# The column transform of the first pass with its weights and data exchanged, and the sums moved two slots on

## The chip, the core and the metric
The kernel runs as one program on 1 core of one Trainium2 chip. Its engines are TensorE (matmuls, into the accumulation memory PSUM), VectorE, ScalarE, GpSimd (POOL in the rows) and SyncE (SP), each with its own instruction queue; they wait for each other by semaphores. Transfers between main memory and on-chip memory run on 16 DMA engines. The metric is the time of one execution on the device in microseconds.

## The reference
The input `x` is 16 images of 64 channels of 256 x 256 fp32. Layer 0 normalizes `x` in groups of two channels, takes a two-dimensional real Fourier transform, keeps 32 x 17 modes of it, mixes the 16 channels of each of 4 heads with complex weights at each mode, transforms back and adds `x`:

```
x_freq = rfft2(gn(x)); xf = x_freq.reshape(B, 4, 16, fH, fW)
core = einsum('bhixy,hioxy->bhoxy', xf[:, :, :, :32, :17], weight)
x = x + irfft2(out_freq) + bias
```

Layer 1 normalizes again, applies a Lorentz-style normalization over the channels, for which it needs means over all images, and adds `x`.

## The kernel before, in words
Three passes run one after the other. Pass A (`stage_a`, lines 145 to 541) reads every image, computes its modes, mixes them and stores the mixed modes and the statistics. Pass B gathers the means over all images; pass C reads `x` a third time and writes the output. The change touches pass A alone.

**Tiles.** An image `b` is 8 tiles `q`, each with two channels of each head (2 MB, two DMAs of 1 MB, `load`, L210). Four buffers `xt` hold tiles, so tile `q` of an image takes the place of tile `q - 4`.

**TensorE, a slot per tile** (`slot`, L298). `row_dft(b, q)` transforms along the rows: 8 matmuls with 64 columns of weights and 512 moving, in pairs that write PSUM partitions 0 to 63 and 64 to 127; the profile has two records for each fp32 matmul. `transposes` then turns the copied rows of tile q-1 (8 records), and `col_dft` makes the modes of tile q-2: 8 matmuls (16 records) whose weights are 128 columns of data and whose moving operand is the 34 columns of the transform matrix, so that the modes come out with (head, row mode) on the partitions, 34 values for each of two channels. In slot 2 of image b TensorE also does `first_sums(b-1)` (two matmuls over squares and mean modes, L278) ahead of the column transform, and `second_sums(b-2)` (over the energy of the mixed modes, L287) at its end.

**ScalarE, a tile at a time** (`tile`, L347). Four activations sum the squares of the tile; between them ScalarE copies the rows (`copy_rows`, L333, two halves) and the transposed rows (`copy_tr`, L339, two halves) out of PSUM. After eight tiles `keep` (L360) copies the sums of squares.

**VectorE** (`entry`, L484). For each q it copies the modes of one tile out of PSUM (`copy_cols`, L384) and does one eighth of the mixing of the image before (`mix`, L390: a product and a reduction). After the eight of image b follow, in this order: `finish(b-1)` (L399: the rotated modes, L404 and L405, then the energy, L406 to L410), `first_norm(b)` (waits for first_sums(b)), `second_norm(b-1)` (waits for second_sums(b-1)) and `start(b)`, which scales the modes that the next eight products use. `mean_sum` (L436) after the first product waits for two powers by GpSimd.

**SP's queue** (L200 to L237) issues everything that is loaded, in program order. In the loop over the images b from 2 on, the store of the mixed modes stands between the loads of tile 3 and tile 4:

```
for q in range(Q):
    if q == 4:
        store_modes(b - 2)
    load(b, q)
```

`store_modes(b - 2)` (L205) begins with a wait for the two instructions L404 and L405 of `finish(b - 2)`. A load waits until TensorE and ScalarE are through with the tile that it overwrites. Waits of SP on register values have line 111.

Of the kernel before, what the change touches and what calls it, by code (L numbers as in the profile page):

```python
# [144 lines left out]
def stage_a(nc, ctx, io, B):  # L145
# [7 lines left out]
    const_in, w_in, neg_w = sem("const_in"), sem("w_in"), sem("neg_w")  # L153
    rows_mm, rows_sb = sem("rows_mm"), sem("rows_sb")
    tr_mm, tr_sb = sem("tr_mm"), [sem(f"tr_sb{i}") for i in range(2)]
    cols_mm, cols_sb = sem("cols_mm"), sem("cols_sb")
    sq_done, sq_kept = sem("sq_done"), sem("sq_kept")
    sums_mm, energy, stat_mm = sem("sums_mm"), sem("energy"), sem("stat_mm")
    y_ready, y_out, st_ready, st_out, chain = sem("y_ready"), sem("y_out"), sem("st_ready"), sem("st_out"), sem("chain")
    sums_read, stat_read = sem("sums_read"), sem("stat_read")  # L160
    var1_ready, rstd1_ready, var2_ready, yrot_out = sem("var1_ready"), sem("rstd1_ready"), sem("var2_ready"), sem("yrot_out")
    chain_end, macc_out, powers = sem("chain_end"), sem("macc_out"), sem("powers")

    with ExitStack() as mem:
# [10 lines left out]
        wm = sb("wm", [128, CI, 2, CI * M2])  # L175
        rows = [[sb(f"rows{a}{i}", [128, 512]) for i in range(2)] for a in range(2)]
        cols = [[sb(f"cols{a}{i}", [128, 512]) for i in range(2)] for a in range(2)]
        junk = [sb(f"junk{k}", [128, 1024], BF16) for k in range(2)]
        sq = sb("sq", [128, Q, HEADS])
        sqk = sb("sqk", [128, Q, HEADS])  # L180
# [8 lines left out]
        st = sb("st", [128, 4, CI])  # L189
        p_rows = [ps(f"p_rows{i}", [128, 512]) for i in range(2)]  # L190
        p_tr = [ps(f"p_tr{i}", [128, 512]) for i in range(2)]
        p_cols = [ps(f"p_cols{a}", [128, 2, M2]) for a in range(2)]
        p_sums = ps("p_sums", [128, 512])
        p_stat = ps("p_stat", [128, 512])
        consts = ((dft_h, "dft_h"), (dft_w, "dft_w"), (sel, "sel"), (mode_w, "mode_w"), (misc, "misc"), (ident, "ident"))

        block = mem.enter_context(nc.Block())
# [41 lines left out]
        @block.tensor  # L239
        def _(pe):  # L240
            def row_dft(b, q):

                pe.wait_ge(x_in[q % NX], b * 64 + (q // NX) * 32 + 32)
                for i in range(2):
                    if not (is_at(b, 0) and q == 0):
                        pe.wait_ge(rows_sb, b * 16 + 2 * q + i - 1)
                    for j in range(2):
                        for t in range(2):
                            last = nc.tensor.matmul(p_rows[i][64 * t:64 * t + 64, :], dft_h[:, j], xt[q % NX][:, t::2, i, j * W:(j + 1) * W],  # L249
                                                    start=(j == 0), stop=(j == 1))  # L250
                    last.then_inc(rows_mm, 1)

            def transposes(b, q):
                for i in range(2):
                    pe.wait_ge(rows_sb, b * 16 + 2 * q + i + 1)
                    if not (is_at(b, 0) and q == 0):
                        pe.wait_ge(tr_sb[i], b * 8 + q)
                    for hl in range(2):
                        for wh in range(2):

                            out = p_tr[i][:].rearrange("p (w r h k) -> p w h r k", w=2, r=2, h=4)[:, wh, 2 * hl:2 * hl + 2]
                            last = nc.tensor.transpose(out, rows[q % 2][i][:, 256 * hl + 128 * wh:256 * hl + 128 * wh + 128], ident[:])
                    last.then_inc(tr_mm, 1)

            def col_dft(b, q):
                if not (is_at(b, 0) and q < 2):
                    pe.wait_ge(cols_sb, b * 8 + q - 1)
                for i in range(2):
                    pe.wait_ge(tr_sb[i], b * 8 + q + 1)
                    v = cols[q % 2][i][:].rearrange("p (w r n) -> p w r n", w=2, r=2)  # L270
                    n = 0
                    for wh in range(2):
                        for r in range(2):
                            last = nc.tensor.matmul(p_cols[q % 2][:, i], v[:, wh, r], dft_w[:, r, wh], start=(n == 0), stop=(n == 3))
                            n += 1
                last.then_inc(cols_mm, 1)

            def first_sums(b):  # L278

                pe.wait_ge(sq_kept, b + 1)  # L280
                pe.wait_ge(cols_sb, b * 8 + 8)
                if not is_at(b, 0):
                    pe.wait_ge(sums_read, b)
                nc.tensor.matmul(p_sums[:, 0:32], sel[:, 0], sqk[:].rearrange("p q h -> p (q h)"), start=True, stop=True)
                nc.tensor.matmul(p_sums[:, 32:48], sel[:, 1], xm[:, :, 0], start=True, stop=True).then_inc(sums_mm, 1)

            def second_sums(b):  # L287

                pe.wait_ge(energy, b + 1)
                if not is_at(b, 0):  # L290
                    pe.wait_ge(stat_read, b)
                nc.tensor.matmul(p_stat[:, 0:16], sel[:, 2], sm[:, 8], start=True, stop=True)
                nc.tensor.matmul(p_stat[:, 16:32], sel[:, 1], y[:, :, 0], start=True, stop=True).then_inc(stat_mm, 1)

            def before(b, q, n):
                return (b, q - n) if q >= n else (b - 1, q - n + Q)

            def slot(b, q):  # L298
                row_dft(b, q)
                transposes(*before(b, q, 1))  # L300
                if q == 2 and not is_at(b, 0):
                    first_sums(b - 1)
                col_dft(*before(b, q, 2))
                if q == 2 and not (is_at(b, 0) or is_at(b, 1)):
                    second_sums(b - 2)

            pe.wait_ge(const_in, 32 + 16 * 8)
            row_dft(0, 0)
            row_dft(0, 1)
            transposes(0, 0)  # L310
            for q in range(2, Q):
                slot(0, q)
            for q in range(Q):
                slot(1, q)
            with pe.Fori(2, B) as b:
                for q in range(Q):
                    slot(b, q)
            transposes(B - 1, Q - 1)
            col_dft(B - 1, Q - 2)
            col_dft(B - 1, Q - 1)  # L320
            first_sums(B - 1)
            second_sums(B - 2)
            second_sums(B - 1)

        @block.scalar
        def _(act):
# [12 lines left out]
            def copy_tr(b, q, i):  # L339
# [4 lines left out]
                    act.wait_ge(cols_mm, b * 8 + q - 1)  # L344
                nc.scalar.activation(cols[q % 2][i][:], p_tr[i][:], ACT.Copy).then_inc(tr_sb[i], 1)

            def tile(b, q):  # L347
                act.wait_ge(x_in[q % NX], b * 64 + (q // NX) * 32 + 32)
                squares(b, q, 0)
                squares(b, q, 1)  # L350
                copy_rows(b, q, 0)
                if not (is_at(b, 0) and q == 0):
                    copy_tr(b, q - 1, 0)
                squares(b, q, 2)
                if not (is_at(b, 0) and q == 0):
                    copy_tr(b, q - 1, 1)
                squares(b, q, 3)
                copy_rows(b, q, 1)
# [11 lines left out]
            with act.Fori(1, B) as b:  # L370
                for q in range(Q):
                    tile(b, q)
                keep(b)
            for i in range(2):
                copy_tr(B - 1, Q - 1, i)

        @block.vector
        def _(dve):
# [2 lines left out]
            pair = lambda a: a.rearrange("p (g i) -> p g i", i=2)  # L381
            V = nc.vector

            def copy_cols(b, q):  # L384
                dve.wait_ge(cols_mm, b * 8 + q + 1)
                if q == 0 and not is_at(b, 0):
                    dve.wait_ge(sums_mm, b)
                V.tensor_copy(xm[:, 2 * q:2 * q + 2], p_cols[q % 2][:]).then_inc(cols_sb, 1)

            def mix(q, waited=None):  # L390

# [67 lines left out]
            def start(b):  # L459
# [8 lines left out]
                ch.step(V.tensor_scalar(row(7, 8), row(7, 8), misc[:, 4:5], None, ALU.mult))  # L468
                dcs = pair(xh[:, 0, 0::2])
                ch.step(V.tensor_tensor(dcs, dcs, row(7, 8).unsqueeze(2).to_broadcast((128, 8, 2)), ALU.add))  # L470
            ch.inc(V.memset(row(20), 0.0))
            ch.inc(V.memset(y[:, :, M2:YS], 0.0))
            ch.inc(V.memset(yrot[:, :, M2:YS], 0.0))
            dve.wait_ge(const_in, 32 + 16 * 8)
            for q in range(Q):
                copy_cols(0, q)
                if q == 5:
                    dve.wait_ge(w_in, 16)
                    neg = wm[:, :, 0].rearrange("p o (n r) -> p o n r", r=2)[:, :, :, 1]
                    ch.inc(V.tensor_scalar(neg, neg, -1.0, None, ALU.mult))  # L480
            first_norm(0)
            start(0)

            def entry(b, last=False):  # L484
                for q in range(Q):
                    copy_cols(b, q)
                    mix(q, None if is_at(b, 1) or q else (b - 1) * 16)
                    if q == 0 and not is_at(b, 1):
                        mean_sum(b - 2)
                finish(b - 1)  # L490
                first_norm(b)
                second_norm(b - 1)
                start(b)
# [48 lines left out]


PER_A = 47

TB = 4096
TC = 2048
# [823 lines left out]
```

## Time and profile before

| | |
|---|---|
| Time, median of 3 runs | 3578.98 us (3571.15 to 3595.31) |
| Profiled execution, its own time | 3573.87 us |
| Its span | 3572.3 us |
| Pass A | about 0 to 1030 us |
| Busy in the span: TensorE, VectorE, ScalarE, GpSimd | 2887.4, 2648.6, 2158.7, 1541.4 us |
| Mean DMA rate | 339 GB/s |
| VectorE's product L394 and its reduction L397 | 128 each, 2416 and 2421 ns |
| TensorE's row transform L249 | 2048 records, 515.7 us busy |
| Squares L330 on ScalarE | 512, 1055 ns each |

In the rows below, a timeline merges equal neighbouring instructions (x8 is eight of them, with their common start and length). A bracket at its end is the idle time of the engine before it and who ended that. PE is TensorE, DVE VectorE, ACT ScalarE. A busy TensorE is not at its peak; its clock is read from the granted share, 1.00 for the full level (2.4 GHz) and 0.50 for half of it.

### The profile page before, as it was taken

To read this page: it belongs to the slowest core of one execution; us is meant where nothing else is said; L and a number is where in the kernel's file an instruction comes from. 1 tells how busy PE (TensorE), PEld (TensorE's weight loads), DVE (VectorE), ACT (ScalarE), POOL (GpSimd) and SP (SyncE) were. 2 spreads that over 40 slices of the span, in tenths; PEclk is the share of its full clock that TensorE was granted. 3 is DMA by queue.
4 is the path that set the end of the run, shared out by engine and by line. 5 is a ranking of instruction groups with operands and counts; after the bars stand their busy time and mean duration, and the time that the engine had idled before them with its cause. 6 is when DMAs were issued, how large, how long until landed. Compare 5 with 4: busy or idle time off the path is not lost. (4 is left out here: it accounts for less than half of the span.)

```text
span 3572.3 us, 69803 instructions
## 1 busy us (share of the span) xinstructions
PE 2887.4 (81%) x26018; PEld 1418.3 (40%) x26018; DVE 2648.6 (74%) x2600; ACT 2158.7 (60%) x2994; POOL 1541.4 (43%) x862
## 2 busy tenths in 40 slices
PE   6999999999617567777671898888888889888887
PEld 3555555555402122222220544444444444444443
DVE  0788888888866635645562698888888888888888
ACT  6998888888500101101110788777787778777777
POOL 0112121111211112112211688777787777777777
PEclk9999999999759788887885899999999999999999
DMA  9888797979349899999994799999999999999998
GB/s 377 298 292 315 276 329 272 330 274 326 126 149 400 314 380 407 397 389 392 400 376 98 289 383 389 368 377 382 376 379 368 374 373 367 377 369 381 378 377 338
DMA packets 293208, 1211.31 MB, mean 339 GB/s; under 512 B 35265, under 2 KB 49798, under 8 KB 210694
## 3 DMA queue, kind: packets, MB, share of 16 engines
q1 hardware_dynamic: 263526, 1152.42, 84.4%
q0 software_dynamic: 14112, 43.37, 3.7%
q10 hardware_dynamic: 15360, 12.60, 1.2%
q8 instruction: 148, 2.42, 0.3%
q14 instruction: 62, 0.51, 0.0%
HBM read 883.89 MB, written 324.31 MB: 338 GB/s over the span
## 5 line engine op out<-in xcount | busy, mean ns | idle before, releaser
L1297 POOL TENSOR_TENSOR c_ot<-c_ot,c_pp 128x1024 f32<-128x1024 f32 x512 | 1214.7, 2374 | 409.7 <-DVE c_ot L1250 408.5
L1240 DVE SCALAR_TENSOR_TENSOR c_xt<-c_xt,keep_k,c_p_u 128x1024 f32<-128x1024 f32 x512 | 653.8, 1277 | 124.8 <-PE c_p_u L1120 97.5
L1250 DVE SCALAR_TENSOR_TENSOR c_ot<-c_p_f,keep_k,c_xt 128x1024 f32<-128x1024 f32 x512 | 657.2, 1284 | 117.8 <-DMA out<-c_ot 69.6
L1194 ACT ACTIVATE c_pp<-c_p_p,keep_cols 128x1024 f32<-128x1024 f32 x512 | 571.2, 1116 | 262.8 <-PE c_p_p L1132 261.4
L1120 PE MATMUL c_p_u<-c_mv,c_zc 64*128 64x256 f32 x4096 | 595.0, 410 | 74.8 <-DVE c_xt L1240 73.0
L1201 ACT ACTIVATE c_sq<-c_xt,keep_cols 128x1024 f32<-128x1024 f32 x512 | 583.3, 1139 | 60.0 <-DVE c_xt L1240 59.8
L330 ACT ACTIVATE a_junk<-a_xt 128x1024 bf16<-128x1024 f32 x512 | 537.7, 1055 | 26.6 <-DMA a_xt<-in_x 19.4
L249 PE MATMUL a_p_rows<-a_xt,a_dft_h 128*64 128x512 f32 x2048 | 515.7, 647 | 36.5 <-DMA a_bias_t<-in_bias 18.5
L1120 PEld LDWEIGHTS c_p_u<-c_mv,c_zc 64*128 64x128 f32 x4096 | 361.1, 190 | 353.8 <-issue 211.2
L1132 PE MATMUL c_p_f<-c_rt,keep_lw 64*128 64x512 bf16 x1024 | 313.0, 386 | 114.1 <-DVE c_ot L1250 101.6
L516 POOL TENSOR_TENSOR a_sm<-a_sm 128x8 f32<-128x8 f32 x16 | 26.8, 1672 | 806.4 <-DVE a_sm L457 806.4
L655 PE MATMUL b_p_al<-b_xt,b_awc 128*32 128x512 f32 x2048 | 292.0, 646 | 102.2 <-DMA b_xt<-in_x 102.0
L1132 PE MATMUL c_p_p<-c_rt,keep_lw 64*128 64x512 bf16 x1024 | 316.3, 390 | 0.0
L397 DVE TENSOR_REDUCE a_y<-a_prod 128x68 f32<-128x2176 f32 x128 | 309.9, 2421 | 5.6
L394 DVE TENSOR_TENSOR a_prod<-a_wm,a_xh 128x2176 f32<-128x2176 f32 x128 | 309.3, 2416 | 0.3
L713 ACT ACTIVATE b_dn<-b_dn,b_minus 128x512 f32<-128x512 f32 x16 | 11.6, 723 | 488.6 <-DVE b_dn L841 488.6
L816 DVE TENSOR_TENSOR b_prod<-b_spt,b_arow 64x2176 f32<-64x2176 f32 x16 | 38.7, 2418 | 335.0 <-DMA b_spt<-spec 334.9
L1143 PE MATMUL c_p_t<-c_sq,c_hw 128*32 128x512 f32 x2048 | 284.9, 629 | 1.3 <-ACT c_sq L1201 1.3
L655 PE MATMUL b_p_ls<-b_xt,b_awc 128*32 128x512 f32 x2048 | 283.4, 628 | 0.0
L1106 PEld LDWEIGHTS c_p_z<-c_idft,c_ys 128*37 128x37 f32 x7936 | 232.3, 114 | 105.6 <-issue 105.6
L1106 PE MATMUL c_p_z<-c_idft,c_ys 128*37 128x64 f32 x7936 | 271.4, 221 | 0.0
L249 PEld LDWEIGHTS a_p_rows<-a_xt,a_dft_h 128*64 128x64 f32 x2048 | 136.4, 147 | 307.9 <-issue 187.9
(205 smaller groups left out, 3032.0 us busy)
## 6 DMA issues: line engine op xcount, KB each, us to landing
a_xt<-in_x SPq DMA_DIRECT2D x256, 1024.0 KB, 8.8
b_xt<-in_x SPq DMA_DIRECT2D x128, 2048.0 KB, 16.8
c_xt<-in_x SPq DMA_DIRECT2D x256, 1024.0 KB, 16.2
out<-c_ot SPq DMA_DIRECT2D x256, 1024.0 KB, 16.5
c_rt<-maps SPq DMA_DIRECT2D x256, 96.0 KB
maps<-b_maps ACTq DMA_DIRECT2D x192, 64.0 KB, 13.5
maps<-b_maps POOLq DMA_DIRECT2D x64, 192.0 KB, 9.4
dmap<-b_dmap POOLq DMA_DIRECT2D x16, 768.0 KB, 13.5
```

The lines of the kernel that those rows point to most:

```text
L249: last = nc.tensor.matmul(p_rows[i][64 * t:64 * t + 64, :], dft_h[:, j], xt[q % NX][:, t::2, i, j * W:(j + 1) * W], start=(j == 0), stop=( ...
L330: nc.scalar.activation(junk[h % 2][:].rearrange("p (i w) -> p i w", i=2), xt[q % NX][:, h], ACT.Square, accum_out=sq[:, q, h:h + 1]).then_ ...
L397: ch.step(V.tensor_reduce(y[:, 2 * q:2 * q + 2, 0:M2].rearrange("p o (a k) -> p o a k", a=2), prod[:].rearrange("p o a (k n) -> p o a k n" ...
L655: last = nc.tensor.matmul(out[32 * j:32 * j + 32, :], awc[:, par, kind, 15 - k:47 - k], xt[t % NX][:, at:at + 512], start=(k == 0), stop=F ...
L1106: last = nc.tensor.matmul(p_z[64 * at:64 * at + YS, 64 * c:64 * c + 64], ys[:, 8 * part + c], idft[:, chunk, at], start=True, stop=True)
L1120: last = nc.tensor.matmul(p_u[:, 512 * at + W * r:512 * at + W * r + W], zc[t // CH][64 * at:64 * at + 64, i], mv[t % NB][64 * at:64 * at ...
L1132: last = nc.tensor.matmul(p[:, 512 * k:512 * k + 512], keep["lw"][at:at + 64, b].rearrange("p c s -> p (c s)"), rt[t % NB][at:at + 64, c:c ...
L1194: S.activation(pp[n][:], p_p[:], ACT.Identity, bias=keep["cols"][:, b, 1:2]).then_inc(pp_done, 1)
L1201: S.activation(sq[t % 2][:, 1024 * n:1024 * n + 1024], xt[t % NB][:, 1024 * n:1024 * n + 1024], ACT.Square, scale=keep["cols"][:, b, 0:1]) ...
L1240: V.scalar_tensor_tensor(out=u, in0=u, scalar=kc, in1=p_u[:], op0=ALU.mult, op1=ALU.add).then_inc(u_done, 1)
L1250: V.scalar_tensor_tensor(out=ot[t % NB][:, at], in0=p_f[:], scalar=kinv, in1=xt[t % NB][:, at], op0=ALU.add, op1=ALU.mult).then_inc(f_done, 1)
L1297: P.tensor_tensor(o, o, pp[n][:], ALU.add).then_inc(o_done, 1)
```

## The change
The column transform now has the 34 columns of the transform matrix as weights and the 128 columns of data moving. The two channels' results go to PSUM partitions 0 to 33 and 64 to 97 of one tile, `p_cm`. As the modes then lie on the partitions, ScalarE copies them (`copy_cm`, 98 partitions x 128), and one transpose per tile, `turn`, brings them back into `p_turn`, four tiles to a buffer. VectorE copies four tiles at once (`copy_half`), twice an image. `first_sums` and `second_sums` move from slot 2 to slot 4, the first of them to the slot's beginning, and the sums share one PSUM buffer. SP's program is not in the diff.

```diff
-            p_cols = [ps(f"p_cols{a}", [128, 2, M2]) for a in range(2)]
-            p_sums = ps("p_sums", [128, 512])
-            p_stat = ps("p_stat", [128, 512])
+            p_cm = ps("p_cm", [128, 512])
+            p_turn = [ps(f"p_turn{a}", [128, 512]) for a in range(2)]
+            p_stats = ps("p_stats", [128, 512])
+            p_sums, p_stat = p_stats[:, 0:64], p_stats[:, 64:96]
...
             def col_dft(b, q):
-                if not (is_at(b, 0) and q < 2):
-                    pe.wait_ge(cols_sb, b * 8 + q - 1)
+                if not (is_at(b, 0) and q == 0):
+                    pe.wait_ge(cm_sb, b * 8 + q)
                 for i in range(2):
                     pe.wait_ge(tr_sb[i], b * 8 + q + 1)
-                    v = cols[q % 2][i][:].rearrange("p (w r n) -> p w r n", w=2, r=2)
-                    n = 0
-                    for wh in range(2):
-                        for r in range(2):
-                            last = nc.tensor.matmul(p_cols[q % 2][:, i], v[:, wh, r], dft_w[:, r, wh], start=(n == 0), stop=(n == 3))
-                            n += 1
+                v = [cols[q % 2][i][:].rearrange("p (w r n) -> p w r n", w=2, r=2) for i in range(2)]
+                n = 0
+                for wh in range(2):
+                    for r in range(2):
+                        for i in range(2):
+                            last = nc.tensor.matmul(p_cm[64 * i:64 * i + M2, 0:128], dft_w[:, r, wh], v[i][:, wh, r],
+                                                    start=(n == 0), stop=(n == 3), skip_group_check=True)
+                        n += 1
                 last.then_inc(cols_mm, 1)
+            def turn(b, q):
+                pe.wait_ge(cm_sb, b * 8 + q + 1)
+                if q % 4 == 0 and not is_at(b, 0):
+                    pe.wait_ge(cols_sb, b * 2 + q // 4 - 1)
+                at = 128 * (q % 4)
+                nc.tensor.transpose(p_turn[q // 4][:, at:at + CM], cm[q % 2][:], ident[0:CM, 0:CM]).then_inc(turn_mm, 1)
             def first_sums(b):
                 pe.wait_ge(sq_kept, b + 1)
-                pe.wait_ge(cols_sb, b * 8 + 8)
+                pe.wait_ge(cols_sb, b * 2 + 2)
                 if not is_at(b, 0):
                     pe.wait_ge(sums_read, b)
+                    if not is_at(b, 1):
+                        pe.wait_ge(stat_read, b - 1)
...
             def second_sums(b):
                 pe.wait_ge(energy, b + 1)
+                pe.wait_ge(sums_read, B if is_at(b, B - 1) else b + 2)
...
             def slot(b, q):
+                if q == 4 and not is_at(b, 0):
+                    first_sums(b - 1)
                 row_dft(b, q)
                 transposes(*before(b, q, 1))
-                if q == 2 and not is_at(b, 0):
-                    first_sums(b - 1)
+                if not (is_at(b, 0) and q < 3):
+                    turn(*before(b, q, 3))
                 col_dft(*before(b, q, 2))
-                if q == 2 and not (is_at(b, 0) or is_at(b, 1)):
+                if q == 4 and not (is_at(b, 0) or is_at(b, 1)):
                     second_sums(b - 2)
...
+            def copy_cm(b, q):
+                if q < 0:
+                    b, q = b - 1, q + Q
+                act.wait_ge(cols_mm, b * 8 + q + 1)
+                if not (is_at(b, 0) and q < 2):
+                    act.wait_ge(turn_mm, b * 8 + q - 1)
+                nc.scalar.activation(cm[q % 2][:], p_cm[0:CM, 0:128], ACT.Copy).then_inc(cm_sb, 1)
             def tile(b, q):
                 act.wait_ge(x_in[q % NX], b * 64 + (q // NX) * 32 + 32)
                 squares(b, q, 0)
+                if not (is_at(b, 0) and q < 3):
+                    copy_cm(b, q - 3)
                 squares(b, q, 1)
...
-            def copy_cols(b, q):
-                dve.wait_ge(cols_mm, b * 8 + q + 1)
-                if q == 0 and not is_at(b, 0):
+            def copy_half(b, half):
+                dve.wait_ge(turn_mm, b * 8 + 4 * half + 4)
+                if half == 0 and not is_at(b, 0):
                     dve.wait_ge(sums_mm, b)
-                V.tensor_copy(xm[:, 2 * q:2 * q + 2], p_cols[q % 2][:]).then_inc(cols_sb, 1)
+                V.tensor_copy(xm[:, 8 * half:8 * half + 8], p_turn[half][:].rearrange("p (n m) -> p n m", m=64)[:, :, 0:M2]).then_inc(cols_sb, 1)
...
             def entry(b, last=False):
                 for q in range(Q):
-                    copy_cols(b, q)
+                    if q == 5:
+                        copy_half(b, 0)
                     mix(q, None if is_at(b, 1) or q else (b - 1) * 16)
                     if q == 0 and not is_at(b, 1):
                         mean_sum(b - 2)
+                copy_half(b, 1)
                 finish(b - 1)
                 first_norm(b)
                 second_norm(b - 1)
```

Before its first copy VectorE zeroes `p_cm`. After the last slot the remaining turns and copies follow in the same order.

## Rows read from the trace of the kernel before

**Rows 1.** Busy time by stretch: start:end, length, PE, PEld, DVE, ACT, POOL, PEclk, DMA share, GB/s

```profile
100.70:906.00 805.30, 767.32 (x4593) 438.02 (x4591) 683.41 (x858) 698.18 (x1359) 135.01 (x53) 0.94 0.83 298
...
391.00:392.00 1.00, 1.00 (x4) 0.24 (x2) 0.86 (x8) 0.00 (x0) 0.63 (x1) 0.50 1.04 404
```

**Rows 2.** Timeline of an ordinary slot, PE and ACT: start, length, engine, line, operation

```profile
402.35 1.09 PE L262 MATMUL a_p_tr<-a_ident,a_rows 128*128 128x128 f32 x8
403.28 1.87 PE L274 MATMUL a_p_cols<-a_dft_w,a_cols 128*128 128x34 f32 x16
405.08 3.68 PE L249 MATMUL a_p_rows<-a_xt,a_dft_h 128*64 128x512 f32 x16
408.69 0.55 PE L262 MATMUL a_p_tr<-a_ident,a_rows 128*128 128x128 f32 x3
...
402.40 0.60 ACT L337 ACTIVATE a_rows<-a_p_rows 128x512 f32<-128x512 f32 x1
403.12 0.60 ACT L345 ACTIVATE a_cols<-a_p_tr 128x512 f32<-128x512 f32 x1
...
406.17 0.60 ACT L337 ACTIVATE a_rows<-a_p_rows 128x512 f32<-128x512 f32 x1
```

**Rows 3.** Timeline of PE, from slot 2 to slot 4

```profile
384.16 1.95 PE L274 MATMUL a_p_cols<-a_dft_w,a_cols 128*128 128x34 f32 x16
388.72 0.60 PE L292 MATMUL a_p_stat<-a_sm,a_sel 128*128 128x16 f32 x2 [2.61 <-DVE a_sm L410]
...
389.68 6.41 PE L249 MATMUL a_p_rows<-a_xt,a_dft_h 128*64 128x512 f32 x16
...
398.75 2.82 PE L249 MATMUL a_p_rows<-a_xt,a_dft_h 128*64 128x512 f32 x12
```

**Rows 4.** Waits of SP's queue, 0 to 1030 us: total, times, longest

```profile
SPq L111 <- DVE a_yrot L405: 231.2, 14, 16.6
```

**Rows 5.** Timeline of SP's queue around the store

```profile
385.26 0.37 SPq L207 DMA_DIRECT2D spec<-a_y  x1
...
386.61 14.50 SPq L215 DMA_DIRECT2D a_xt<-in_x  x8
...
387.20 0.42 SPq L215 DMA_DIRECT2D a_xt<-in_x  x1
```

**Rows 6.** DMA issues at 386.61 and at 387.20: last number, us to landing

```profile
a_xt<-in_x SPq DMA_DIRECT2D x1, 1024.0 KB, 6.2
...
a_xt<-in_x SPq DMA_DIRECT2D x1, 1024.0 KB, 8.3
```

**Rows 7.** Timeline of DVE, from `finish` to the second product

```profile
384.41 0.36 DVE L404 TENSOR_SCALAR a_yrot<-a_y,a_misc 128x272 f32<-128x272 f32 x1
...
389.79 0.17 DVE L415 TENSOR_REDUCE a_sm<-a_p_stat 128x8 f32<-128x16 f32 x1
...
400.76 2.42 DVE L394 TENSOR_TENSOR a_prod<-a_wm,a_xh 128x2176 f32<-128x2176 f32 x1
```

**Rows 8.** Group by line and shape, 0 to 760 us: busy us, mean ns

```profile
L388 DVE COPY a_xm<-a_p_cols 128x68 f32<-128x68 f32 x100 | 22.9, 229 | 172.1 <-PE a_p_cols L274 163.1 <-DVE a_xh L470 6.2
```

**Rows 9.** Timeline: first sums and product, first and 15th `finish`, two neighbouring products

```profile
100.84 0.31 PE L284 MATMUL a_p_sums<-a_sqk,a_sel 128*128 128x32 f32 x2
...
106.70 2.42 DVE L394 TENSOR_TENSOR a_prod<-a_wm,a_xh 128x2176 f32<-128x2176 f32 x1
...
153.17 0.36 DVE L404 TENSOR_SCALAR a_yrot<-a_y,a_misc 128x272 f32<-128x272 f32 x1
...
962.48 0.36 DVE L404 TENSOR_SCALAR a_yrot<-a_y,a_misc 128x272 f32<-128x272 f32 x1
...
977.96 2.43 DVE L394 TENSOR_TENSOR a_prod<-a_wm,a_xh 128x2176 f32<-128x2176 f32 x1
...
982.88 2.42 DVE L394 TENSOR_TENSOR a_prod<-a_wm,a_xh 128x2176 f32<-128x2176 f32 x1
```

**Rows 10.** Timeline of PE, a row transform after a long pause

```profile
55.70 6.14 PE L249 MATMUL a_p_rows<-a_xt,a_dft_h 128*64 128x512 f32 x16 [12.48 <-DMA a_xt<-in_x]
```

More of the change, by code:

```diff
@@ L155, in stage_a @@
     tr_mm, tr_sb = sem("tr_mm"), [sem(f"tr_sb{i}") for i in range(2)]
-    cols_mm, cols_sb = sem("cols_mm"), sem("cols_sb")
+    cols_mm, cm_sb, turn_mm, cols_sb = sem("cols_mm"), sem("cm_sb"), sem("turn_mm"), sem("cols_sb")
     sq_done, sq_kept = sem("sq_done"), sem("sq_kept")
@@ L159, in stage_a @@
     y_ready, y_out, st_ready, st_out, chain = sem("y_ready"), sem("y_out"), sem("st_ready"), sem("st_out"), sem("chain")
+    cm_zero = sem("cm_zero")
     sums_read, stat_read = sem("sums_read"), sem("stat_read")
@@ L177, in stage_a @@
         cols = [[sb(f"cols{a}{i}", [128, 512]) for i in range(2)] for a in range(2)]
+        cm = [sb(f"cm{a}", [CM, 128]) for a in range(2)]
         junk = [sb(f"junk{k}", [128, 1024], BF16) for k in range(2)]
@@ L298, in slot @@
             def slot(b, q):
+                if q == 4 and not is_at(b, 0):
+                    first_sums(b - 1)
                 row_dft(b, q)
                 transposes(*before(b, q, 1))
-                if q == 2 and not is_at(b, 0):
-                    first_sums(b - 1)
+                if not (is_at(b, 0) and q < 3):
+                    turn(*before(b, q, 3))
                 col_dft(*before(b, q, 2))
-                if q == 2 and not (is_at(b, 0) or is_at(b, 1)):
+                if q == 4 and not (is_at(b, 0) or is_at(b, 1)):
                     second_sums(b - 2)
             pe.wait_ge(const_in, 32 + 16 * 8)
+            pe.wait_ge(cm_zero, 1)
             row_dft(0, 0)
@@ L317, in _ @@
                     slot(b, q)
+            turn(B - 1, Q - 3)
             transposes(B - 1, Q - 1)
             col_dft(B - 1, Q - 2)
+            turn(B - 1, Q - 2)
             col_dft(B - 1, Q - 1)
+            turn(B - 1, Q - 1)
             first_sums(B - 1)
@@ L373, in _ @@
                 keep(b)
+            copy_cm(B - 1, Q - 3)
             for i in range(2):
                 copy_tr(B - 1, Q - 1, i)
+            copy_cm(B - 1, Q - 2)
+            copy_cm(B - 1, Q - 1)
         @block.vector
@@ L470, in start @@
                 ch.step(V.tensor_tensor(dcs, dcs, row(7, 8).unsqueeze(2).to_broadcast((128, 8, 2)), ALU.add))
+            V.memset(p_cm[:], 0.0).then_inc(cm_zero, 1)
             ch.inc(V.memset(row(20), 0.0))
@@ L474, in _ @@
             dve.wait_ge(const_in, 32 + 16 * 8)
[L475 to L480, printed above, removed]
+            copy_half(0, 0)
+            dve.wait_ge(w_in, 16)
+            neg = wm[:, :, 0].rearrange("p o (n r) -> p o n r", r=2)[:, :, :, 1]
+            ch.inc(V.tensor_scalar(neg, neg, -1.0, None, ALU.mult))
+            copy_half(0, 1)
             first_norm(0)
@@ L544 @@
 PER_A = 47
+CM = 64 + M2
 TB = 4096
```

## The prediction, made before the change was run

> **What bounds the kernel now.** I read the stretches first, to see where the change can act at all. The first pass over the images, the only code that the diff touches, ends at about 1030 us of 3572.3 (table above). In its steady part TensorE is busy 767.3 of 805.3 us, ScalarE 698.2 and VectorE 683.4, while the DMA share is 0.83: three engines are close together and none has much to give [rows 1]. The other two passes start after it and keep their time, so only the first pass moves.
>
> Next, one ordinary slot in order of time. TensorE goes straight through transposes (402.35), the column transform (403.28), row transform (405.08) and the next transposes (408.69): 6.34 us a slot. ScalarE closes a ring with it: its last copy of a tile starts at 406.17, lasts 0.60 and releases the second half of the next row transform; transposes follow, then ScalarE's copy out of them, the one at 403.12 one slot earlier. From 403.12 to the end at 406.77 is 3.65 us; the other 2.7 of the 6.34 are TensorE's half row transform and first transposes [rows 2]. Eight slots are 50.7 us.
>
> An image takes longer than that. From the first VectorE `finish` at 153.17 to that of image 14 at 962.48 there are 14 rounds, (962.48 - 153.17) / 14 = 57.81 us each [rows 9]. The timeline around one `finish` shows the missing 7 us: after the column transform (384.16 + 1.95 = 386.11) TensorE waits 2.61 us for VectorE's energy sum, then the next row transform takes 6.41 us instead of 3.68, at a granted clock of 0.50 [rows 1 to 3]. That is the wait that the change attacks by moving the sums two slots on.
>
> The view that decides is the wait list of SP's queue, which no engine's busy time shows. In 14 of 14 loop images SP stands 16.5 us at the store of the modes and waits for the second instruction of `finish` (L405) [rows 4]. Behind that store, in the same queue, stands the load of tile 4 of the running image. Today `finish` of image b-2 begins at 384.41, in TensorE's slot 2 of image b; the store goes out at 385.26, the tile's two loads at 386.61 and 387.20 [rows 5, 7]. They land 6.2 and 8.3 us later, the second at 395.50 [rows 6], and row transform 4 starts at 398.75 [rows 3]: 3.25 us to spare, so the wait is hidden.
>
> **The change, part by part.**
>
> Column transform: 16 records in 1.80 us (403.28 to 405.08) go; in their place 8 fp32 matmuls with 34 columns of weights and 128 moving, in two column halves of the array. The row transform's pairs do this with 512 moving: 16 records in 3.6 us, so a quarter of the columns is 0.9 us if the pairs run side by side, and 1.8 us if they don't or if weights bind as now [rows 2]. I take 1.0, nearest to the row of the same form. One transpose (`turn`) is an eighth of 0.93 us, 0.12 [rows 2]. TensorE saves some 0.7 us a slot, but this is off the ring through ScalarE described above: nothing in the time of a slot.
>
> ScalarE: one copy of 128 columns a tile. 512 columns take 0.60 us [rows 2]; a quarter of them lies between 0.15 and 0.60, and I take 0.3, about 0.2 after the overlap between neighbours. The copies at 402.40 and 403.12 start 0.72 us apart and the first needs under 0.5 of it (406.17 plus 0.60, less the overlap), so the gap hides it; if that cover is gone, a slot grows by up to 0.2 us, 1.6 an image. It is covered again below, as ScalarE will stand idle for tile 4.
>
> VectorE: eight copies of 0.23 us go, two copies of 272 elements come. An instruction of that size, L404, takes 0.36 [rows 7, 8]; bounds 0.23 and twice 0.36. The products no longer wait for single columns.
>
> **The sums, the step that decides.** `first_sums(b-1)` now stands ahead of row transform 4 of image b and waits for `copy_half(b-1, 1)`. VectorE issues this after all eight products, right before `finish(b-2)`. Queued behind first_sums on TensorE is row transform 4. That one also needs tile 4, whose loads are behind `store_modes(b-2)` in SP's queue, which waits for that same `finish(b-2)`. The diff leaves SP's program alone. So TensorE and ScalarE come to tile 4 when its loads are not even issued; the 3.25 us to spare turn into the whole latency. `second_sums(b-2)` stands at the end of this slot, and VectorE cannot go on to `second_norm`, `start` and the next eight products without it. That makes a ring, whose length I add up from rows:
> - `finish` begins to tile 4 there: 384.41 to 395.50 = 11.1 us [rows 5 to 7].
> - Row transform 4 at half clock after such a pause: 6.1 us, as after the pause of 12.48 us at 55.70 (6.14); 6.41 after 2.61 us of waiting; 3.68 at full clock [rows 2, 3, 10]. Transposes 0.8, turn 0.1, columns 1.0, and the two sum matmuls until VectorE goes on: 1.07 us today at half clock (388.72 to 389.79), 0.6 at full; I take 0.7. Together 8.7 [rows 2, 3, 7].
> - VectorE from there to its second product: 389.79 to 400.76 = 10.97, less a column copy of 0.23, is 10.74 (the mean sum's wait for GpSimd lies inside). Seven more products at 982.88 - 977.96 = 4.92 are 34.4. Two half copies at 0.36 are 0.7. Together 45.9 [rows 7 to 9].
>
> The ring is 11.1 + 8.7 + 45.9 = 65.7 us, against 57.8 now. The other engines need 8 x 6.34 + 0.5 for ScalarE's keeping of the squares + 2.7 for the half clock = 54, so they wait some 11 us an image (0.5 is an estimate for one small copy and its wait); they are not the bound.
>
> How often: the loads of images 0 and 1 have no store ahead of them. `first_sums(0)` moves from 100.84 two slots later less the slack, to 108.7; first product 5.9 us later, as 106.70 is after 100.84; eight products and 0.7: first `finish` at 108.7 + 5.9 + 39.4 + 0.7 = 154.7, 1.5 later than now. Then 14 rounds: 154.7 + 14 x 65.7 = 1074.5, against 962.48. What follows (last products, norms, stores) has nothing of the change in it but copies. So +112 us: 3573.9 + 112 = 3686 in the terms of the profiled execution, which is 5.1 below the median of the runs shown. I forecast 3690, 3.1% slower.
>
> **A rule against a row.** The load's landing is a large term. The two rows give 8.9 us from the first issue to the second landing. The Trainium skill, DMA: Bandwidth & Descriptors, section Anatomy of one DMA, fits about 2.0 us plus the bytes over 436 GB/s. Two loads of 1 MB would by that fit be there after 6.8 us, an estimate from that page, and the ring would be 63.6. The page measured another issuing path, and the first load alone already takes 6.2 us here, so the rows are taken.
>
> **The rivals.**
> 1. *Faster: the store does not hold the load.* If tile 4 were there, only VectorE's ring would count: first_sums 0.5, row transform 3.6, 0.8 + 0.1 + 1.0 + 0.7, and 45.9 = 52.6 us; 14 rounds end at 891, 71 us early: 3508 for the median, or 3546 with the row transform at half clock (+2.7 a round). It decides if `finish(b-2)` begins more than 11.1 us before TensorE comes to slot 4. For it: today it does, by 14.3 us (384.41 to 398.75). Against: the new order puts both behind the same copy of columns, and SP's wait is in all 14 images [rows 3, 4, 7]. 6%.
> 2. *The column pairs don't overlap, or ScalarE and the half copies cost their upper bounds.* +0.8 for the columns, up to +0.7 for the half copies, 0.3 for the clock: 66.6 to 67.5, which is 3703 to 3715. For: 128-column weights are the bound of a record today [rows 2]; against: 34 columns load less. 13%.
> 3. *The second load takes 6.2 us too,* as nothing else moves then: it lands 2.1 us earlier, 29 us in 14 rounds, 3661. For: the first row; against: both loads share the engines and the second row says 8.3 [rows 6]. 6%.
> 4. *The clock doesn't fall:* row transform 3.68, -2.4 a round, 3656. Against it both pauses in rows 3 and 10. 4%.
> 5. My own case, 3675 to 3702: 71%.
>
> **How the numbers follow.** The unknowns of my case are the columns (-0.1 to +0.4), the half copies (-0.3 to +0.3), the stat matmuls and the clock (-0.6 to +0.5): about 1 us a round, 14 us. Cases 3 and 4 below and 2 above bring the range to 3654 to 3710. This kernel's runs tell 1% (36 us) from no change; slower by that means over 3615. Slower 0.92; within 1% 0.03, for a mix in which some rounds go free; faster 0.05 from rival 1.
>
> **What would show it.** SP's wait for L405 grows from 16.5 to about 27 us in 14 images. TensorE waits some 10 us for `a_xt` ahead of row transform 4, ScalarE too, ahead of a square; by the rows today neither can, with 3.25 us to spare. `finish` to `finish` 65.7 us. Ordinary slots stay at 6.3 us with column records of about 1 us in sum. VectorE waits for the stat matmuls at about 15 us a round. First pass ends at about 1142. If slots 4 show no wait for a load, the prediction is wrong in its main step; if the rounds are 57.8 or less, VectorE's ring was mis-read.

## The result and the profile after

The changed kernel takes 3703.95 us (median of 4 runs, 3667.81 to 3709.72) against 3581.63 for the kernel before: ratio 1.032, 95% interval 1.024 to 1.039, slower. The forecast was 3690, range 3654 to 3710.

SP's queue first. These are its waits in the first pass of the changed kernel, total, times and longest:

```profile
SPq L111 <- DVE a_yrot L440: 347.4, 14, 25.3
```

It is the row of [rows 4] again, 231.2 us in 14 waits before, now 347.4 in 14, 24.8 each: tile 4's load stands longer behind the store. Next, what TensorE and VectorE wait for in the steady part, 160 to 900 us:

```profile
DVE a_sm L450 <- PE a_p_stats L309: 162.1, 12, 13.8
ACT a_junk L352 <- DMA a_xt<-in_x: 122.2, 12, 11.1
PE a_p_rows L252 <- DMA a_xt<-in_x: 119.2, 12, 10.7
...
PE a_p_stats L299 <- DVE a_xm L423: 21.6, 11, 2.0
```

TensorE and ScalarE now each wait about 10 us for a tile in every one of the 12 images seen (TensorE 5.7 us in the first, 10.1 to 10.7 in the others), and VectorE 13.5 us for the second sums (L309), which stand behind that tile. The last row is the wait for the half copy ahead of the first sums, 2.0 us. Stretches of the same kernel, with columns as in [rows 1], show what that costs, and the clock behind such a wait:

```profile
160.00:900.00 740.00, 557.83 (x3831) 270.91 (x3831) 552.39 (x656) 577.23 (x1196) 119.21 (x48) 0.89 0.75 272
424.00:426.00 2.00, 1.98 (x6) 0.76 (x8) 0.00 (x0) 1.99 (x4) 0.00 (x0) 0.50 1.05 385
426.00:428.00 2.00, 2.00 (x8) 0.54 (x8) 0.00 (x0) 0.77 (x3) 0.00 (x0) 0.69 1.05 386
```

TensorE is busy for 75% of the time, where it was 95% [rows 1], and VectorE for 75% as well: no engine is busy throughout, the time goes to waiting for each other. One round in order of time shows the ring. SP's timeline:

```profile
413.79 0.37 SPq L210 DMA_DIRECT2D spec<-a_y  x1
414.34 0.36 SPq L211 DMA_DIRECT2D spec<-a_yrot  x1
415.14 25.43 SPq L218 DMA_DIRECT2D a_xt<-in_x  x12
```

TensorE's:

```profile
410.12 1.07 PE L279 MATMUL a_p_cm<-a_cols,a_dft_w 128*34 128x128 f32 x16
413.16 0.40 PE L299 MATMUL a_p_stats<-a_sqk,a_sel 128*128 128x32 f32 x2 [1.98 <-DVE a_xm L423]
413.40 0.43 PE L300 MATMUL a_p_stats<-a_xm,a_sel 128*128 128x16 f32 x2
424.02 5.23 PE L252 MATMUL a_p_rows<-a_xt,a_dft_h 128*64 128x512 f32 x16 [10.19 <-DMA a_xt<-in_x]
429.19 1.09 PE L265 MATMUL a_p_tr<-a_ident,a_rows 128*128 128x128 f32 x8
...
431.54 0.38 PE L309 MATMUL a_p_stats<-a_y,a_sel 128*128 128x16 f32 x2
431.84 3.67 PE L252 MATMUL a_p_rows<-a_xt,a_dft_h 128*64 128x512 f32 x16
```

And VectorE's:

```profile
412.59 0.44 DVE L423 COPY a_xm<-a_p_turn 128x272 f32<-128x272 f32 x1
412.95 0.35 DVE L439 TENSOR_SCALAR a_yrot<-a_y,a_misc 128x272 f32<-128x272 f32 x1
...
431.95 0.18 DVE L450 TENSOR_REDUCE a_sm<-a_p_stats 128x8 f32<-128x16 f32 x1 [13.54 <-PE a_p_stats L309]
...
442.38 2.42 DVE L429 TENSOR_TENSOR a_prod<-a_wm,a_xh 128x2176 f32<-128x2176 f32 x1
...
477.74 0.35 DVE L439 TENSOR_SCALAR a_yrot<-a_y,a_misc 128x272 f32<-128x272 f32 x1
```

`finish` begins at 412.95, right behind the half copy (412.59) that TensorE's first sums wait for; the store goes out at 413.79, the tile's loads at 415.14, the tile is there at 424.02; before, `finish` began at 384.41 and slot 4 at 398.75, with 3.25 us to spare [rows 3, 5, 7]. VectorE gets its sums at 431.95 and comes to the next `finish` at 477.74. A round is now (1061.04 - 153.11) / 14 = 64.85 us, from the first and the 15th `finish`, against 57.81 [rows 9]. The column transform itself did what it should: 1.07 us for its 16 records where it was 1.87 [rows 2].

The first pass ends 98.6 us later (1061.04 against 962.48 at the 15th `finish`). The whole profiled span grew by 126.7 us. The other 28 lie behind the first pass. Here is the first instruction of pass B that needs its inputs and the matmul of pass C's main loop, each with its count, shortest, median and longest in ns, first and last start, in the kernel before:

```profile
L900 DVE TENSOR_SCALAR b_mrow<-b_mrow x1: 196/196/196, 1048.5 to 1048.5; 128x64 f32<-128x64 f32 x1
...
L1120 PE MATMUL c_p_u<-c_mv,c_zc x4096: 376/376/793, 1985.1 to 3559.2; 64*128 64x256 f32 x196
```

And in the changed kernel:

```profile
L938 DVE TENSOR_SCALAR b_mrow<-b_mrow x1: 197/197/197, 1147.2 to 1147.2; 128x64 f32<-128x64 f32 x1
...
L1158 PE MATMUL c_p_u<-c_mv,c_zc x4096: 376/376/793, 2112.1 to 3685.9; 64*128 64x256 f32 x196
```

From the one to the other pass B took 1985.1 - 1048.5 = 936.6 us and 2112.1 - 1147.2 = 964.9. In the twelve experiments, all with the same pass B, it took 931 to 986. Pass C's loop, from its first matmul to its last, took 1574.1 us before and 1573.8 after. So single executions can differ by 1% for nothing that was changed. The profiled execution of e7 below, with the longest pass B (986 us), is also the slowest of that kernel's five (3539.78 us, median 3508.97). This is why I read the rounds below and not the times alone.

### The profile page after: what moved, and what is told of

Read it like the earlier page. It is cut to its first block and busy times, and to the rows that moved or that the text cites. A ratio compares the mean times of both kernels' runs of the same rounds, so it can differ in the third digit from the quotient of the medians.

```text
span 3699.0 us, 70294 instructions
## 1 busy us (share of the span) xinstructions
PE 2795.2 (76%) x26146; PEld 1293.8 (35%) x26146; DVE 2643.9 (71%) x2505; ACT 2172.3 (59%) x3122; POOL 1535.8 (42%) x862
## 6 DMA issues: line engine op xcount, KB each, us to landing
a_xt<-in_x SPq DMA_DIRECT2D x256, 1024.0 KB, 10.1
```

## The experiments

Times are medians; the ratio is to the kernel before, run on the same chip. "Round" is the distance of the first to the 15th `finish`, divided by 14, from each kernel's trace, so of one execution each.

| Kernel | us | ratio, interval | round, us |
|---|---|---|---|
| before | 3581.63 | | 57.8 |
| changed | 3703.95 | 1.032, 1.024 to 1.039 | 64.9 |
| e1 changed, store behind tile 7 | 3539.78 | 0.986, 0.979 to 0.992 | 54.7 |
| e2 changed, store ahead of tile 5 | 3559.25 | 0.987, 0.978 to 0.996 | 55.0 |
| e3 changed, store ahead of tile 3 | 3802.88 | 1.060, 1.052 to 1.068 | 71.7 |
| e4 changed, sums in slot 3 | 3589.82 | 0.998, 0.994 to 1.003 | 56.6 |
| e5 before, store behind tile 7 | 3676.43 | 1.025, 1.020 to 1.030 | 64.7 |
| e6 before, sums in slot 3, store behind 7 | 3570.73 | 0.997, 0.994 to 1.001 | 57.0 |
| e7 e1 with early second sums | 3508.97 | 0.977, 0.971 to 0.982 | 51.7 |
| e8 e4 with the store behind tile 7 | 3614.14 | 1.007, 1.002 to 1.011 | 59.0 |
| e9 e4 with the store ahead of tile 5 | 3533.94 | 0.986, 0.982 to 0.990 | 54.5 |
| e10 before, sums in slot 3, store ahead of 5 | 3520.27 | 0.981, 0.976 to 0.987 | 53.9 |
| e11 before, store ahead of tile 5 | 3577.42 | 1.001, 0.997 to 1.004 | 57.8 |
| e12 e7 with the store ahead of tile 5 | 3549.51 | 0.988, 0.981 to 0.995 | 53.3 |

**e1: take the store out of the load's way.**

```diff
                 for q in range(Q):
-                    if q == 4:
-                        store_modes(b - 2)
                     load(b, q)
+                store_modes(b - 2)
```

> The changed kernel, with the store of the modes moved behind the load of tile 7 in SP's queue; nothing else differs. Main theory (tile 4's load stands behind a store that waits for finish): the wait of TensorE for a_xt in the loop goes, and the round falls from 64.85 us to VectorE's own ring, 52.6 us if the clock holds through row transform 4 and up to 55.5 if it does not; 14 rounds are 130 to 170 us, so 3535 to 3575, below the kernel before. Rival 'the sums come too late by themselves' (VectorE waits for sums at the end of slot 4 whatever the loads do): the round stays above 60, over 3630. Rival 'the new columns cost it': no change, 3700.

Measured 3539.78, round 54.7. TensorE's wait for tiles is gone from the steady part. With nothing but SP's order changed, the median falls by 164 us, below the kernel before. Of these the rounds account for 142: the 15th `finish` begins at 919.2 instead of 1061.04. The round is not at 52.6, because the clock still falls in most rounds. TensorE's timeline around slot 4:

```profile
425.45 1.07 PE L278 MATMUL a_p_cm<-a_cols,a_dft_w 128*34 128x128 f32 x16
428.45 0.40 PE L298 MATMUL a_p_stats<-a_sqk,a_sel 128*128 128x32 f32 x2 [1.93 <-DVE a_xm L422]
428.69 0.37 PE L299 MATMUL a_p_stats<-a_xm,a_sel 128*128 128x16 f32 x2
428.99 5.35 PE L251 MATMUL a_p_rows<-a_xt,a_dft_h 128*64 128x512 f32 x16
```

And two stretches of it, the granted clock third from the end:

```profile
429.00:431.00 2.00, 2.00 (x7) 0.77 (x8) 1.93 (x4) 1.92 (x5) 0.00 (x0) 0.51 0.78 247
431.00:433.00 2.00, 2.00 (x8) 0.51 (x6) 1.90 (x7) 0.33 (x1) 0.00 (x0) 0.64 1.03 383
```

Behind a wait of only 1.93 us the clock stands at 0.51, and row transform 4 takes 5.35 us instead of 3.67: 1.7 us a round, and 52.6 + 1.7 = 54.3. Eleven of the 14 rounds are at 54.5 or 54.6. The second round shows the other case: after a wait of 1.78 us (to 211.88) the clock stays at 1.00, row transform 4 takes 3.65 us, and the round is 52.9.

**e2 and e3: move the store by one tile either way** (`q == 5`, `q == 3` in place of `q == 4`).

> The changed kernel, with the store one tile later, ahead of the load of tile 5 instead of tile 4. Main theory: tile 5 lands 11.1 us after finish begins, TensorE comes to slot 5 some 7 to 9 us after it, so 2 to 4 us of waiting stay in slot 5, but behind second_sums and off VectorE's ring: round 52.6 to 55.5, like the kernel with all loads first, 3535 to 3575. Rival 'any load behind the store costs its whole latency': 3700 still.

> The changed kernel, with the store one tile earlier, ahead of the load of tile 3. Main theory: slot 3 now waits for its tile and the whole of slot 3 is added to the ring: 11.1 to the landing, slot 3 with the falling clock 7.3, slot 4 at full clock 6.8 with both sums, 45.8 on VectorE, together 71.0 us; 14 rounds x 6.1 us more than the changed kernel, about 3790. Rival 'only the latency of one load counts, wherever it stands': 64.9 a round, 3704. Rival 'the sums come too late by themselves': 64.9.

Measured: 55.0 and 71.7 us a round, 3559 and 3803. In e2 TensorE waits 2.4 us for tile 5 in 12 images, as foreseen, and the round is nearly that of e1. For e3 the sum had said 71.0. What is between the awaited tile and the second sums counts, not the latency alone:

```profile
525.42 5.56 PE L252 MATMUL a_p_rows<-a_xt,a_dft_h 128*64 128x512 f32 x16 [19.67 <-DMA a_xt<-in_x]
...
533.57 3.67 PE L252 MATMUL a_p_rows<-a_xt,a_dft_h 128*64 128x512 f32 x16
...
539.52 0.38 PE L309 MATMUL a_p_stats<-a_y,a_sel 128*128 128x16 f32 x2
```

Two slots, 525.42 to 539.9, now lie in the ring. That rules out that the late sums alone cost the time: in e1, e2, e3 and the changed kernel they stand in the same place.

**e4: the sums in slot 3** (`q == 3` in place of `q == 4` at both sums), the store as in the changed kernel.

> The changed kernel with both sums in slot 3 instead of slot 4, and the store where it was. Main theory: second_sums no longer stands behind tile 4. Tile 4 is there 11.1 us after finish begins, TensorE waits 2 to 4 us for it, but the ring goes through two images: one way 51.5 to 53.5 us (eight slots), the other 45.8 + 11.1 = 56.9, mean 54.2 to 55.2 us a round; 135 to 150 us less than the changed kernel, 3555 to 3570, below the kernel before. Rival 'the new columns, the turn and the copy cost it': no better than the changed kernel, 3700. Rival 'the wait for tile 4 costs its 10 us wherever the sums stand': above 60 a round, over 3630.

Measured 3589.82, round 56.6: a miss of 1.4 to 2.4 us. The main claim holds, no 10 us are lost, but the sum left out a ring. Waits in the steady part:

```profile
DVE a_xm L423 <- PE a_p_turn L289: 49.8, 16, 5.0
PE a_p_rows L252 <- DMA a_xt<-in_x: 49.4, 13, 4.7
```

TensorE waits 3.8 us for tile 4, and VectorE waits for the turn of tile 7, in slot 2. So `finish`, and with it the load, hangs on TensorE's slot 2, and eight slots of TensorE, the wait and the half clock after it add up: 8 x 6.26 = 50.1, 3.8, and 1.3 to 2.9 for a row transform of 5.0 to 6.6 us instead of 3.67, together 55.2 to 56.8. Two more kernels test this.

> The changed kernel with the sums in slot 3 and loads first. It tells why the kernel with the sums in slot 3 alone needed 56.9 us a round and not 54.2 to 55.2. If the 3.2 to 3.8 us of waiting for tile 4 and the half clock after it are the difference: no wait for a_xt here, 52.5 to 54.6 a round, about 3530. If the sums in slot 3 are too early for VectorE (it waits for the turn of tile 7 in slot 2): 56 to 57 still, about 3570.

e8 came out at 3614.14 and 59.0 us, outside of what either theory gave. A wait that neither had counted was in it, VectorE's for the store; e5 below tells of it:

```profile
DVE a_y L431 <- DMA spec<-a_y: 53.3, 13, 4.6
```

e9 was made to have neither that wait nor the one for the tile:

> The changed kernel with the sums in slot 3 and the store ahead of the load of tile 5: tile 4 is not behind the store, and the store is not behind tile 7 either. In the kernel with the sums in slot 3 and all loads first, VectorE waited 4.1 us a round for that late store. Theory: without both waits the round is VectorE's ring, 6.8 to 8.5 us on TensorE and 45.8 on VectorE, 52.6 to 54.6 us: about 3535. Rival 'sums in slot 3 are too early for VectorE, which waits for the turn of tile 7': 56 to 57, about 3580.

e9: 3533.94, round 54.5, no wait for a tile and none for a turn in its steady part. So the wait for tile 4, with what follows from it, was the 2 us: only the place of the store differs from e4. And its 54.5 with the 4.1 us that VectorE waits for the store in e8 make 58.6, near e8's 59.0.

**e5: the same move of the store in the kernel before.**

> The kernel before, with only the store moved behind the load of tile 7. Main theory: there the store's wait is hidden (3.25 us to spare at slot 4), so the round stays 57.8 us and the time the same, 3580 within the spread. Rival 'the place of the store is a cost of its own, in any order of the sums': some us a round less, under 3550.

Measured 3676.43, round 64.7: both theories failed, the kernel is 2.5% slower. VectorE's timeline around the first reduction of a round:

```profile
346.17 0.36 DVE L403 TENSOR_SCALAR a_yrot<-a_y,a_misc 128x272 f32<-128x272 f32 x1
...
356.60 2.42 DVE L393 TENSOR_TENSOR a_prod<-a_wm,a_xh 128x2176 f32<-128x2176 f32 x1
371.23 2.42 DVE L396 TENSOR_REDUCE a_y<-a_prod 128x68 f32<-128x2176 f32 x1 [12.21 <-DMA spec<-a_y]
```

And SP's store of `y`:

```profile
362.96 0.37 SPq L207 DMA_DIRECT2D spec<-a_y  x1
```

The reduction overwrites `y`, which the store must have read. Here `finish` ends in slot 2, but the load of tile 7, ahead of the store, waits for row transform 3 and its squares. The store goes out at 362.96, 16.8 us after `finish` began at 346.17, and VectorE goes on only at 371.23, another 8.3 us later. In the changed kernel the sums, and with them `finish`, come later in TensorE's order, and the same place of the store cost nothing (no such wait in e1). A store in a load queue can be too early for the loads and too late for its buffer. e11 tests whether one tile's delay is free:

> The kernel before with the store ahead of the load of tile 5. Behind the load of tile 7 it cost 7 us a round, since VectorE then waited for the store to overwrite y. Theory: one tile later changes nothing, as both the wait for tile 4 and the store have time to spare: 58.0 us a round, the same time. If the load of tile 4 had been a hidden limit, under 57; if any delay of the store costs, over 59.

e11: 3577.42, 57.8: unchanged, so both waits are hidden in the kernel before at tile 4 and at tile 5.

**e6 and e10: are the new columns worth anything?** Both are the kernel before with its old column transform and the sums in slot 3:

```diff
             def slot(b, q):
+                if q == 3 and not is_at(b, 0):
+                    first_sums(b - 1)
                 row_dft(b, q)
                 transposes(*before(b, q, 1))
-                if q == 2 and not is_at(b, 0):
-                    first_sums(b - 1)
                 col_dft(*before(b, q, 2))
-                if q == 2 and not (is_at(b, 0) or is_at(b, 1)):
+                if q == 3 and not (is_at(b, 0) or is_at(b, 1)):
                     second_sums(b - 2)
```

> The kernel before with its old column transform, the sums moved from slot 2 to slot 3 (slot 4 would deadlock there: column transform 2 waits for a copy that VectorE makes after it has the sums) and all loads ahead of the store. Main theory (the gain lies in giving VectorE time before the sums are wanted, the column exchange itself is off the path): energy is ready before TensorE asks, the wait of 2.61 us and the half clock go, eight slots of 6.34 and the extras make 52.4 to 54.6 us a round, as good as the changed kernel with loads first: 3510 to 3540. Rival 'the faster columns are what the loads-first kernel gains by': the round stays 57 to 58, about 3580.

e6: 3570.73, round 57.0, a miss for the main theory as it stood. The late store is in it again: VectorE waits 45.1 us in 13 reductions for it. With the store ahead of tile 5:

> The kernel before with its old columns, the sums in slot 3 and the store ahead of the load of tile 5. With all loads first it needed about 57 us a round, of which VectorE waited 3.5 for the late store. Theory 'later sums are the gain, the columns are not': 52.4 to 54.6 us a round, 3520 to 3540, like the best of the new-column kernels with the sums in slot 4. Rival 'the new columns and half copies give the gain, because the old copies keep VectorE and TensorE in step': 56 to 58 a round, 3570 or more.

e10: 3520.27, round 53.9, against 3533.94 and 54.5 for the same order with the new columns (e9). The two intervals overlap. So with the sums in slot 3 the column exchange, with its copy and its turn, brings nothing that can be measured. The later sums do: from e11 to e10 they alone move, and the round goes from 57.8 to 53.9. For slot 4 the question stays open. The old columns were not run with the sums there, nor in the order of e7 below.

Rounds 2 to 6 of e10 are at 52.8 or 52.9, most later ones at 54.5 or 54.6, with the same program. TensorE's timeline shows what differs. In 12 of the 14 rounds it waits 0.64 to 0.70 us for a copy by VectorE ahead of the columns in slot 4:

```profile
378.03 1.97 PE L274 MATMUL a_p_cols<-a_dft_w,a_cols 128*128 128x34 f32 x16 [0.65 <-DVE a_xm L388]
379.94 3.65 PE L249 MATMUL a_p_rows<-a_xt,a_dft_h 128*64 128x512 f32 x16
...
430.90 2.21 PE L274 MATMUL a_p_cols<-a_dft_w,a_cols 128*128 128x34 f32 x16 [0.64 <-DVE a_xm L388]
433.04 5.06 PE L249 MATMUL a_p_rows<-a_xt,a_dft_h 128*64 128x512 f32 x16
```

At first the clock stays at 1.00 behind it (380 to 382). Later, first behind the wait at 430.90, it falls (0.52 in 434 to 436), and the row transform takes 5.06 to 5.35 us instead of 3.65. That is the 1.7 us between the two lengths of a round. The row transform at 433.04 lies in round 6, but behind its sums, so its delay first shows in round 7. A row transform at half clock is in most rounds of e9 too, so a small difference between the two kernels' columns could hide behind it.

**e7 and e12: the version that beats both.**

```diff
                 row_dft(b, q)
+                if q == 4 and not (is_at(b, 0) or is_at(b, 1)):
+                    second_sums(b - 2)
                 transposes(*before(b, q, 1))
...
                 col_dft(*before(b, q, 2))
-                if q == 4 and not (is_at(b, 0) or is_at(b, 1)):
-                    second_sums(b - 2)
```

> The changed kernel with loads first, and second_sums right behind row transform 4, ahead of the transposes, turn and columns of that slot. Main theory: VectorE's ring loses transposes, turn and columns, 1.9 us, and the half-clock part shrinks; from the 54.6 us of the loads-first kernel the round goes to 51.3 to 52.7, where eight slots of 6.26 and the keeping are the bound: 25 to 45 us less than that kernel, 3500 to 3520. Rival 'TensorE and ScalarE set the 54.6': no change.

e7, with all loads first: 3508.97, ratio 0.977, round 51.7; twelve of its 14 rounds lie at 51.0 to 51.5, as foreseen. By its time it can't be told from e10, as the intervals overlap. TensorE doesn't pause before the first sums, and row transform 4 is at full clock:

```profile
414.70 1.07 PE L278 MATMUL a_p_cm<-a_cols,a_dft_w 128*34 128x128 f32 x16
415.70 0.41 PE L298 MATMUL a_p_stats<-a_sqk,a_sel 128*128 128x32 f32 x2
415.94 0.37 PE L299 MATMUL a_p_stats<-a_xm,a_sel 128*128 128x16 f32 x2
416.25 3.67 PE L251 MATMUL a_p_rows<-a_xt,a_dft_h 128*64 128x512 f32 x16
419.85 0.40 PE L307 MATMUL a_p_stats<-a_sm,a_sel 128*128 128x16 f32 x2
```

> The changed kernel with second_sums right behind row transform 4 and the store ahead of the load of tile 5. With all loads first this order needed 51.3 us a round, the bound of eight slots; a few waits for the store were in it. Theory: 51.3 us again, or up to 53 if tile 5, which lands 11.1 us after finish begins, is waited for (slot 5 comes 7 to 8 us after it, so about 3 us of waiting, which here is on the path as TensorE is the bound): 3500 to 3530. So no better than all loads first.

e12: 3549.51, round 53.3, a miss: the time lies above the 3500 to 3530 expected and the round just above the 53. TensorE has this wait in 11 slots:

```profile
PE a_p_rows L252 <- DMA a_xt<-in_x: 27.1, 11, 3.9
```

As expected, tile 5 is now the one that comes late. Seven of the waits, one in every second image, are 3.5 to 3.9 us, the other four 0.2 to 0.45. The rounds alternate in the same way, at 51.3 to 51.7 and at 54.5 or more. Why only every second image has the long wait, the runs don't show. Two of the long ones:

```profile
436.12 3.65 PE L252 MATMUL a_p_rows<-a_xt,a_dft_h 128*64 128x512 f32 x16 [3.63 <-DMA a_xt<-in_x]
...
859.78 5.35 PE L252 MATMUL a_p_rows<-a_xt,a_dft_h 128*64 128x512 f32 x16 [3.88 <-DMA a_xt<-in_x]
```

The clock stays at 1.00 behind the first and falls to 0.50 behind the second (862 to 864).

## Why the prediction was right

- **The step that decides** (first sums ahead of a tile whose load waits for `finish` in SP's queue): shown. The wait for tile 4 is in every steady round of the changed kernel, and the order of SP's queue alone turns it off (e1) or makes it larger (e3).
- **The ring, 65.7 us**: measured 64.85. `finish` to the tile 11.1 foreseen, 424.02 - 412.95 = 11.07 measured. Tile to sums 8.7 foreseen, 431.95 - 424.02 = 7.93 measured; the term that was too large is the row transform at half clock, 5.23 us and not 6.1, since the clock came back earlier within it (0.69 in 426 to 428, above). VectorE 45.9 foreseen, 477.74 - 431.95 = 45.79 measured. Two terms of it were off against each other: to the second product 10.43 instead of 10.74, the next seven products 34.64 instead of 34.4. The half copies were 0.36 each from start to start, as priced.
- **The first `finish`**: 153.11 measured, 154.7 foreseen. The first sums came at 107.25, not 108.7; TensorE was already ahead in slot 3, whose row transform began at 100.89, against 103.09 before.
- **The sum, +112 us**: the first pass gave +98.6. So the sum was 13 us too large, 0.85 us a round and 1.5 for the first `finish`. The measured median, 3703.95, lies above 3690 all the same, since pass B took 28 us more in the profiled run; with a pass B as before, 3573.9 + 98.6 + 5 would be 3678. The ring and its terms were right; that the forecast came within 14 us of the median is in part luck, as two deviations that have nothing to do with each other went opposite ways.
- **Column transform 1.0 us, off the path**: 1.07 measured. A slot went from 6.34 to 6.26 us (422.84 less 416.58 in e4's trace), where I had said nothing would change; small, and hidden by the ring. TensorE now waits 0.49 us for ScalarE's copy of the rows in such a slot, so ScalarE holds the slot, as foreseen. ScalarE's new copy takes 0.28 us (0.3 foreseen), the turn 0.17 to the next instruction (0.12 foreseen).
- **SP's wait, about 27 us**: 24.8. **VectorE's wait for the sums, about 15**: 13.5.
- **Rival 1** (52.6 us a round, or 2.7 more at half clock) was the state without the store in the way. e1 made it and found 54.7, between the two, as the clock was at half for a part of the row transform only. Rivals 2 to 4: the pairs overlap (1.07 us for 16 records), the tile is there 8.88 us after the first issue where the rows said 8.9, and the clock falls (0.50 in 424 to 426).
- **The rule on the DMA's fixed part** (2.0 us and the bytes over 436 GB/s, fitted to transfers that GpSimd issues; the Trainium skill, DMA: Bandwidth & Descriptors, section Anatomy of one DMA), by which the tile would land 2.1 us sooner: from the first load at 415.14 to the tile at 424.02 it is 8.88 us here, not 6.8. The row was the better price.

## What to carry to other kernels

Before a wait is moved in one engine's order, look up what the released work stands behind in every other queue: here a store waited for the same instruction as TensorE, and the next load stood behind the store. Price a store's place in a load queue from both sides, by the load behind it and by the buffer that it must leave free, and move it together with the work that it follows. When runs spread by 1% through a pass that isn't touched, compare the length of a round in the traces.

## What the runs showed of the hardware that I had not expected

- TensorE's clock fell behind waits shorter than the 2.61 us of the kernel before [rows 1, 3]: 1.93 us in e1 (0.51 in the next 2 us) and 0.64 us in e10 (0.52). The length of the wait alone doesn't tell: it stayed at 1.00 behind 1.78 us in e1's second round, behind 0.64 to 0.70 us in rounds 2 to 5 of e10 and behind 3.63 us in e12. What decides it, the runs don't show.
- One such fall costs a round about 1.7 us where TensorE is in the ring: 52.9 and 54.6 us in e1, 52.9 and 54.6 in e10. In e7 no row transform of the steady part was slowed by it, and the round was 51.3.
- A store issued behind loads in SP's queue lands late. The store of the rotated modes (L208 or L211) took 2.6 us from issue to landing in the kernel before, 8.4 in e1, 8.7 in e5 and 8.8 in e8 (medians), where it stands behind the load of tile 7. For the store of `y`, which VectorE waits for, it was 2.2 us at 385.26 in the kernel before and 8.2 us at 362.96 in e5.
